# More features looked up on TensorE, fewer gathered, in a DLRM interaction tower

## The reference

```python
e = jnp.stack([tbl_0[ids[:, 0]], ..., tbl_26[ids[:, 26]]], axis=1)    # (2048, 27, 128)
dots = jnp.einsum('bnd,bmd->bnm', e, e)
r, c = np.tril_indices(27, k=-1)
h = jnp.concatenate([dots[:, c, r], dense_ctx], axis=1)               # (2048, 367)
h = jnp.maximum(h @ W_top1 + b_top1, 0.0)                             # 512
h = jnp.maximum(h @ W_top2 + b_top2, 0.0)                             # 256
y = h @ W_top3                                                        # (2048, 1)
```

## Time and profile before

| | before |
|---|---|
| median of 3 runs | 397.31 us (397.29 to 397.81) |
| profiled execution | 396.33 us |
| its span | 394.4 us |
| mean granted TensorE clock | 0.97 of full speed |
| busy: PE, DVE, ACT, POOL | 325.2, 251.2, 148.8, 276.4 us |
| matmuls of look-ups, L415 | 1152 |
| indirect gathers, L386 | 288 |

### The profile page before, as it was taken

The page is one execution under the profiler, slowest core; times in us unless marked ns, Lnnn a source line. Parts: engine busy times, 40 slices in busy tenths (PEclk is TensorE's granted clock), DMA queues, the critical chain, the costliest instruction groups (busy, mean ns, idle before and its releaser), DMA issues.

```text
span 394.4 us, 13599 instructions
## 1 busy us (share of the span) xinstructions
PE 325.2 (82%) x5928; PEld 289.8 (73%) x5928; DVE 251.2 (64%) x518; ACT 148.8 (38%) x406; POOL 276.4 (70%) x295
## 2 busy tenths in 40 slices
PE   0751989998998799997989989898889889799947
PEld 0741979887787687896778877697778777797836
DVE  3744995997657836696656856686755856741531
ACT  2251434453433433433433343342533343343421
POOL 6777677777777777777777777777777777777200
PEclk9995799999999989999999999999999999999987
DMA  7996276343433323332533333332423333222100
GB/s 166 248 228 148 73 190 141 95 109 70 91 77 84 83 70 80 87 89 62 96 75 81 88 73 79 80 91 67 97 68 83 81 76 68 57 55 58 29 2 2
DMA packets 23990, 35.48 MB, mean 90 GB/s; under 512 B 7936, under 2 KB 17832, under 8 KB 23932
## 3 DMA queue, kind: packets, MB, share of 16 engines
q0 software_dynamic: 9216, 18.89, 23.1%
q1 hardware_dynamic: 14716, 15.73, 14.8%
HBM read 34.59 MB, written 0.01 MB: 88 GB/s over the span
## 4 chain that ended last, share of the span: by engine, by line
POOL 45%; PE 21%; issue 17%; DMA 9%; SPq 3%; DVE 3%; ACT 1%; DVEq 0%
POOL rows L386 45%; PE e_banks L415 8%; DMA ids_wide<-in_ids 5%; DMA rows<-in_tbl,idx 4%; PE w_bank L476 4%; PE g_banks L446 3%; PE e_banks L427 3%; PE w_bank L487 3%; SPq L339 2%; PE w_bank L465 1%; DVE one_hot L550 1%; DVE zt L561 1%; DVE h L246 1%; SPq L329 1%; ACT et L265 0%
## 5 line engine op out<-in xcount | busy, mean ns | idle before, releaser
L386 POOL DMA_INDIRECT rows<-in_tbl,idx x288 | 275.6, 957 | 91.4 <-issue 85.1
L550 DVE TENSOR_TENSOR one_hot<-ids_wide,row_no 125x1024 fp32r<-125x1024 int32 x144 | 168.5, 1216 | 94.1 <-PE e_banks L415 78.0
L415 PE MATMUL e_banks<-one_hot,table_hi 125*128 125x256 f32 x576 | 153.8, 303 | 27.6 <-DVE table_lo L541 24.3
L415 PE MATMUL e_banks<-one_hot,table_lo 125*128 125x256 f32 x576 | 146.6, 290 | 0.0
L415 PEld LDWEIGHTS e_banks<-one_hot,table_hi 125*128 125x128 f32 x576 | 114.2, 198 | 31.2 <-issue 28.4
L415 PEld LDWEIGHTS e_banks<-one_hot,table_lo 125*128 125x128 f32 x576 | 114.7, 199 | 0.0
L265 ACT ACTIVATE et<-e_banks 128x256 f32<-128x256 f32 x72 | 45.1, 626 | 121.7 <-PE e_banks L415 121.7
L256 ACT ACTIVATE et<-e_banks 128x512 f32<-128x512 f32 (+1 forms) x96 | 51.2, 551 | 45.7 <-PE e_banks L427 45.2
L427 PE MATMUL e_banks<-ident,rows 128*128 128x128 f32 x288 | 46.1, 279 | 22.4 <-DMA rows<-in_tbl,idx 22.4
L446 PEld LDWEIGHTS g_banks<-et 128*26 128x26 f32 x4096 | 43.5, 103 | 16.8 <-issue 13.8
L446 PE MATMUL g_banks<-et 128*26 128x26 f32 x4096 | 52.2, 191 | 3.6 <-issue 2.4
(11 more groups left out here) (19 smaller groups left out, 63.8 us busy)
## 6 DMA issues: line engine op xcount, KB each, us to landing
ids_wide<-in_ids SPq DMA_DIRECT2D x72, 125.0 KB
rows<-in_tbl,idx POOLq DMA_INDIRECT x288
et<-in_tbl SPq DMA_DIRECT2D x9, 448.0 KB
w<-in_W_top SPq DMA_DIRECT2D x2, 256.0 KB
w<-in_W_top SPq DMA_DIRECT2D x1, 512.0 KB
et<-in_tbl SPq DMA_DIRECT2D x9, 52.0 KB
w<-in_W_top SPq DMA_DIRECT2D x1, 222.0 KB
idx<-in_idx SPq DMA_DIRECT2D x1, 202.5 KB, 3.0
```

The lines of the kernel that those rows point to most:

```text
L386: pool.indirect_dma_start(rows[:, k % RING, a, :], None, tables[f], bass.IndirectOffsetOnAxis(ap=idx[:, t, f:f + 1], axis=0)).then_inc(row ...
L415: last = nc.tensor.matmul(e_bank[n % E_BANKS][:, 0:UNIT], part[:, q, c, :], one_hot[:, hot_slot(o, piece), c % PIECE, :], start=(c == 0 an ...
L550: nc.vector.tensor_tensor(one_hot[:, hot_slot(o, piece), :, :], ids_wide[:, o % IDS_RING, :].unsqueeze(1).broadcast_to([OP, PIECE, UNIT]), ...
```

## The change

- Eleven features are looked up (7 and 16 are new) and sixteen gathered, in four chunks of four a tile; the ring of chunks has seven places. A tile is four ticks.
- Features are renumbered in `et`: gathered ones first, looked-up ones behind them, so that each chunk is drained by one copy. The pitch of a sample in `et` is 27 elements in place of 32. The order of the pairs in `h` follows, and W_top1's rows are permuted to it outside the kernel, where the kept tables are padded to 128 partitions of eight rows and stacked as well.
- The triangle is cut into seven rectangular blocks in place of 26 rows: three are copied on ScalarE, four on VectorE.
- `z`, `zt` and `a2` are single, no longer double.
- The drains of H and L1 are all on ScalarE, but for the last unit.
- Each table is one DMA. The eleven ids of unit 0 are issued beside their tables; seven of them land in space of `a1T` and `hT` that is not yet in use. The second part of `idx` comes behind the third table.
- The schedule: look-ups of a unit are spread over ticks ahead of its tiles, grams go two steps to a tick, and H follows the turn of its second tile by one tick.

```diff
-ONE_HOT = (3, 4, 14, 19, 22, 23, 24, 25, 26)
-LOOK_UP_AT = (-5, -4, -3, -2, 0, 1, 2, 3, 4)
+LOOKED_UP = (3, 4, 7, 14, 16, 19, 22, 23, 24, 25, 26)
+GATHERED_IN = ()
-RING = 6
+RING = 7
...
+def pair_blocks(NF):
+    blocks = []
+    half = 1 << (NF - 1).bit_length() - 1
+    while half:
+        whole = [a for a in range(0, NF, 2 * half) if a + 2 * half <= NF]
+        if whole:
+            blocks.append((len(whole), half, half, half, 0, 2 * half))
+        rest = len(whole) * 2 * half
+        if rest + half < NF:
+            blocks.append((1, NF - rest - half, half, rest + half, rest, 0))
+        half //= 2
+    return blocks
...
+    AHEAD = 2
+    FIRST = [("OH", 0, q) for q in looked_up(0)[:AHEAD]]
+    for n, q in enumerate(looked_up(0)[AHEAD:]):
+        put(n * TILE_AT[PAIR] * 7 // 8 // FIRST_LOOK_UPS, ("OH", 0, q))
+    LOOK_UPS_FROM = [0] + [TILE_AT[PAIR * u] * 3 // 4 for u in (1, 2)] + [TILE_AT[PAIR * (u - 1)] + 2 for u in range(3, UNITS + 1)]
     for u in range(1, UNITS):
+        first, next_first = LOOK_UPS_FROM[u:u + 2]
+        for n, q in enumerate(looked_up(u)):
+            put(first + n * (next_first - first) // len(looked_up(u)), ("OH", u, q))
     for t in range(LAST_TILE - 1):
-        at = CHUNKS * (t + 1)
-        for p in range(G_PIECES):
-            put(at + p, ("G", t, p))
-        put(at + G_PIECES, ("turn", t), ("pack", t))
-    for u in range(LAST - 1):
-        at = PAIR * CHUNKS * (u + 1) + CHUNKS
-        layers(u, BOTH, at + 2, (at + 3, at + 4, at + 4, at + 4), at + 9)
+        at = TILE_AT[t + 1] + (2 if t == 0 else 0)
+        put(at, ("G", t, 0), ("G", t, 1))
+        put(at + 1, ("G", t, 2), ("G", t, 3), ("turn", t), ("pack", t))
+    for u in range(LAST):
+        at, then = TILE_AT[PAIR * (u + 1)] + 2, TILE_AT[PAIR * (u + 1) + 1] + 2
+        put(at, *[("H", u, c, BOTH) for c in range(KC)], ("L1", u, 0, BOTH))
+        put(at + 1, ("L1", u, 1, BOTH), ("L1", u, 2, BOTH), ("L1", u, 3, BOTH))
+        put(then - 2 * (u == LAST - 1), ("L2", u, 0))
+        put(then + 1 - 3 * (u == LAST - 1), ("L2", u, 1))
...
-        et = sb("et", [P, ET_TILES, P, STRIP])
-        z = sb("z", [P, PAIR, STRIP, NP])
-        zt = sb("zt", [P, PAIR, NP, STRIP])
+        et = sb("et", [P, ET_TILES, P, NF])
+        z = sb("z", [P, STRIP, NP])
+        zt = sb("zt", [P, NP, STRIP])
...
-            return "act" if s[2] % 2 == 0 else "dve"
+            return "dve" if s[1] == LAST and s[2] % 2 == 1 else "act"
...
-            for q in range(NOH):
-                if q < IDS_RING:
-                    load_ids(q)
-                load_table(q)
+            for n, q in enumerate(TABLE_ORDER):
+                if n < FIRST_LOOK_UPS:
+                    load_ids(n)
+                load_table(n)
+                if n == 2:
+                    sp.dma_start(idx[:, 1:TILES, :], idx_in[:, 1:TILES, :]).then_inc(idx_rest, 16)
+            for o in range(FIRST_LOOK_UPS, FIRST_LOOK_UPS + IDS_RING):
+                load_ids(o)
...
             def turn_tile(t):
                 dve.wait_ge(g_drained, 2 * (t + 1))
+                if t > 0:
+                    dve.wait_ge(act_packed, (KC - 1) * t)
+                    dve.wait_ge(dve_packed, t)
```

More of the change, by code:

```diff
@@ L39, in dlrm_tower @@
     assert B % UNIT == 0 and TILES > ET_TILES
[L41 to L46, removed]
+    assert kept_tables.shape[0] == P and OC % PIECE == 0
     PIECES = OC // PIECE
@@ L61, in dlrm_tower, with looked_up, places_gathered @@
     LAST_TILE = TILES - 1
[L64 to L79, removed]
+    ORDER = feature_order(NF)
+    GATHERED = NF - NOH
+    def looked_up(u):
+        return range(1 if u in GATHERED_IN else 0, NOH)
+    def places_gathered(t):
+        return GATHERED + (t // PAIR in GATHERED_IN)
+    PLACES = {}
+    for t in range(TILES):
+        n = places_gathered(t)
+        parts = -(-n * P // BANK)
+        sizes = [n // parts + (i < n % parts) for i in range(parts)]
+        for i in range(parts):
+            PLACES[t, i] = range(sum(sizes[:i]), sum(sizes[:i + 1]))
+    CHUNKS = list(PLACES)
+    CHUNK_AT = {chunk: k for k, chunk in enumerate(CHUNKS)}
+    TICKS = len(CHUNKS)
+    TILE_AT = [CHUNK_AT[t, 0] for t in range(TILES)] + [TICKS]
+    LOOK_UPS = [(u, q) for u in range(UNITS) for q in looked_up(u)]
+    LOOK_UP_NO = {look_up: o for o, look_up in enumerate(LOOK_UPS)}
+    FIRST_LOOK_UPS = len(looked_up(0))
     BOTH = (0, 1)
@@ L122, in dlrm_tower @@
+    put(at, *[("G", t, p) for p in range(G_PIECES)], ("turn", t), ("pack", t))
+    put(at + 2, *[("H", LAST, c, (0,)) for c in range(KC)], *[("L1", LAST, m, (0,)) for m in range(M1)])
+    put(at + 3, ("L2", LAST, 0))
+    put(TICKS, *[("G", LAST_TILE, p) for p in range(G_PIECES)], ("turn", LAST_TILE), ("pack", LAST_TILE),
+        *[("H", LAST, c, (1,)) for c in range(KC)], *[("L1", LAST, m, (1,)) for m in range(M1)], ("L2", LAST, 1))
     RANK = ("G", "OH", "turn", "pack", "H", "L1", "L2")
@@ L144, in h_turned @@
         return W_AT["H", u, KC - 1, w_tiles(u, j)] + 1
+    BLOCKS, at = [], 0
+    for block in pair_blocks(NF):
+        BLOCKS.append((at, block))
+        at += block[0] * block[1] * block[2]
+    assert at == PAIRS
+    ACT_BLOCKS = sum(at < 2 * P for at, _ in BLOCKS)
+    FIRST_COLUMN = BLOCKS[0][1][3] - 1
+    assert BLOCKS[0][1][0] == 1 and BLOCKS[1][0] >= P
     dense_v = dense_ctx.rearrange("(u j p) c -> p u j c", j=PAIR, p=P)
@@ L230, in rows_landed @@
         def rows_landed(k):
-            return 16 * sum(len(FEATS[c % CHUNKS]) for c in range(k % RING, k + 1, RING))
+            return 16 * sum(len(PLACES[CHUNKS[c]]) for c in range(k % RING, k + 1, RING))
         def hot_slot(o, piece):
@@ L249, in drain_t @@
             _, t, i = s
[L250 to L257, removed]
+            n, at = E_AT[s], PLACES[t, i]
+            act.wait_ge(t_filled, CHUNK_AT[t, i] + 1)
+            nc.scalar.activation(et[:, t % ET_TILES, :, at[0]:at[-1] + 1],
+                                 e_bank[n % E_BANKS][:, 0:len(at) * P].rearrange("p (f b) -> p b f", b=P), ACT.Copy
+                                 ).then_inc(e_drained[n % E_BANKS], 1)
         def drain_look_up(act, s):
@@ L276, in drain_grams @@
                                  ).then_inc(g_drained, 1)
[L279 to L316, removed]
-                nc.vector.tensor_scalar(out, cols, b1[:, m:m + 1], 0.0, ALU.add, ALU.max
-                                        ).then_inc(w_drained[n % WB], 1)
+        def pack_block(eng, j, at, block):
+            count, columns, rows_of, first_column, first_row, step = block
+            first = zt[:, first_column - 1:first_column - 1 + columns, first_row:first_row + rows_of]
+            out = h[:, j, at:at + count * columns * rows_of]
+            if count == 1:
+                return copy(eng, out.rearrange("p (c r) -> p c r", r=rows_of), first)
+            if rows_of == 1:
+                src = zt[:, :, :].rearrange("p c r -> p (c r)")
+                src = src[:, (first_column - 1) * STRIP + first_row:][:, ::step * (STRIP + 1)]
+                return copy(eng, out, src[:, 0:count])
+            whole = zt[:, :, :].rearrange("p c r -> p (c r)")
+            return copy(eng, out.rearrange("p (k c r) -> p k c r", c=columns, r=rows_of), diagonal(whole, block))
@@ L384, in _ @@
                     pool.wait_ge(t_filled, k - RING + 1)
-                for a, f in enumerate(FEATS[i]):
+                for a, place in enumerate(PLACES[t, i]):
+                    f = ORDER[place]
                     pool.indirect_dma_start(
@@ L614 @@
     placed = ids.reshape(B // P, QUADS, STRIP, NF)
-    arrays = {"in_" + name: np.ascontiguousarray(inputs[name]) for name in inputs if name not in ("ids", "b_top1")}
+    order = feature_order(NF)
+    on_chip = LOOKED_UP if not GATHERED_IN else LOOKED_UP[1:]
+    kept = ["ids", "b_top1", "W_top1"] + [f"tbl_{f}" for f in on_chip]
+    arrays = {"in_" + name: np.ascontiguousarray(inputs[name]) for name in inputs if name not in kept}
     arrays["in_idx"] = np.ascontiguousarray(placed.transpose(2, 1, 0, 3)).reshape(P, B // P, NF)
@@ L618 @@
     arrays["in_b1"] = np.ascontiguousarray(np.asarray(inputs["b_top1"]).reshape(-1, P).T)
+    tables = np.stack([np.asarray(inputs[f"tbl_{f}"]) for f in LOOKED_UP])
+    tables = np.pad(tables, ((0, 0), (0, P * OC - tables.shape[1]), (0, 0)))
+    arrays["in_kept_tables"] = np.ascontiguousarray(tables.reshape(len(LOOKED_UP), P, OC, -1).transpose(1, 0, 2, 3))
+    w1 = np.asarray(inputs["W_top1"])
+    pairs = [sorted((order[a], order[b])) for a, b in pair_order(NF)]
+    w1_rows = [b * (b - 1) // 2 + a for a, b in pairs] + list(range(len(pairs), w1.shape[0]))
+    arrays["in_w1"] = np.ascontiguousarray(w1[w1_rows])
     nc = bacc.Bacc("TRN2", target_bir_lowering=False, num_devices=1)
```

283 lines of the change are left out of this document (179 added, 104 removed).

## The result

The changed kernel takes 387.78 us (386.12 to 388.44, four runs) against 397.3: a ratio of 0.9752, interval 0.972 to 0.9785. Measured again, with later experiments, it took 389.1 us, 0.9809 (0.9769 to 0.9849); so where two kernels were not measured together, a difference of half a per cent says nothing. It is faster, as forecast, and inside the range, but by 9.5 us where 20 were forecast. The profiled execution took 386.12 us with a span of 384.3.

The account below looks back on a forecast made before the run. POOL's gathers were taken to bound the kernel, PE close behind. PE's path of 315.3 us, +24.7 for look-ups, -4.0, -5.1, -7.8, -0.9, gave 322.2; with 4 for stalls, 48 of start and the median's distance, 377 us; range 366 to 391.

Parts of the forecast that it names:

- pack and turn: Tile's turn and pack before H: 3.6 us on DVE and ACT, covered by PE's 4.2 us in all units but the first.
- the step on transposes and chunks: Four chunks a tile for five: 38 fewer transposes, -4.0 us, and 30 fewer gram boundaries at 0.17 us each, -5.1 us.
- if a gram step is over 0.9 us: One of the signs given in advance that would show the prediction wrong: a gram step on PE over 0.9 us.
- its 0.77 us: Gram step on PE, taken from start to start at 0.77 us, with no change from the new pitch.
- The tail: End of the kernel: about 21 us before, 0.9 us less through a shorter last pack; a tail of 20 us expected.
- the step on layers: H and L1 drains move to ACT except in the last unit; the wait at L1 costed at zero, -7.8 us.
- the drains of the e banks: In ACT's queue: what stands behind a waiting pack; the pack was held covered, by 0.6 us only.
- the L1 wait: PE's last L1 step of a unit waits 1.26 us for a DVE drain behind one-hots, 7.8 us in all; expected gone.
- The 4 us added for stalls: Allowance on PE's path since row-wait slack is gone; from 52 to 90 us PE idled 1.7 us of 38.
- The case of helpers that starve PE: Rival: lateness of DVE's one-hots or ACT's drains falls on PE, +10 to +17 us, 387 to 394 us; chance 0.20.
- the start's bound by transfer: End of unit 0's eleventh look-up by transfer: 7.26 MB there at 46 us, plus 1.1 + 1.2 + 2.1, given as 50.7 us.
- the chance of the range: Chance given to 366 to 391 us, the forecast plus the starved case's lower half: about 0.75 to 0.8.

Follow-up runs that it names:

- f4: Changed kernel without the matmuls of the tables' lower parts, so looked-up embeddings are only the upper parts: 358.19 us, 0.9029 of the kernel before.
- h2: Changed kernel with features 7 and 16 gathered again, nine looked up and eighteen gathered, in five chunks a tile: 393.03 us, 0.9904 of the kernel before.
- e1: Changed kernel with a look-up put between the two gram steps of a tick: 386.3 us, 0.9721 of the kernel before.
- e2: Changed kernel with all four gram steps of a tile in one tick: 415.33 us, 1.0463 of the kernel before.
- h1: Changed kernel with H's third chunk and L1's first step a tick later, and long matmuls mixed into the tail's grams: 379.86 us, 0.9541 of the kernel before.
- f3: Changed kernel with the drains of L1's second and fourth step on DVE again, H still on ACT: 388.96 us, 0.9791 of the kernel before.
- e3: Changed kernel with H's middle chunk drained by DVE again, layer 1 still on ACT: 416.8 us, 1.0517 of the kernel before.
- g4: Changed kernel with the weights loaded two ticks later, measured in the state of long pauses: 0.9234 of the kernel before.

## Why the prediction was off by half the gain

Right: PE took over from POOL, as f4 shows; row waits went; the start ended at 48.4 us for 48; 77 look-ups cost 149 us for 150.5; pack and turn kept their cover. The move of work from gathers to look-ups gains by itself 1.0 to 1.5% (h2), as much as all the rest of the change or more.

Wrong, in the step on transposes and chunks: "each such boundary costs 0.17 us", booked as -5.1 us for 30 fewer of them. With its waits a gram step cost 0.965 us before (57.9 us by 60) and 1.0 us after; the waits in front of single steps came back inside the pairs. The term measures +2.2 us, not -5.1: this is the largest miss, 7.3 us in a total of 10.7. e1 shows that the placing matters little up to pairs (0 to 3.5 us), e2 that it does beyond. The prediction's own sign, "if a gram step is over 0.9 us", was met, but the kernel before met it already: its 0.77 us left out part of the waits. The tail, with four steps in a row, was sized at 20.2 us and took 22.4.

Wrong, in the step on layers: "on ACT only 0.4 to 0.7 us drains stand in front". Three stood there, behind a pack; H cost 3.9 us more. The prediction named "the drains of the e banks" as what waits behind a pack, and not H's own. h1 gives this back and more.

Right in size for the wrong reason: the L1 wait of 7.8 us went, but f3 shows that the choice of engine is not why. The prediction had misread the wait: the drain stood behind a turn and its packs, and not behind one-hots alone, and the new order moved the turn.

The 4 us added for stalls were not met: transposes and L1 took 2.0 us more and look-ups and L2 2.2 less. They hid as much of the misses above. The rest is 0.4 us of start, 0.6 of the median's distance from the span, and rounding.

The case of helpers that starve PE had the right place (ACT behind the pack), but that place gave 3.9 us where the case had 10 to 17. That its time, 387 to 394 us, fits is luck, and so is that the range holds the measured time: most of the miss is in grams and tail, which the case does not name. Two small sums of the prediction are off: the start's bound by transfer adds up to 50.4 us, not 50.7, and the chance of the range, 0.62 and half of 0.20, is 0.72, not 0.75 to 0.8.

## What to carry to other kernels

A saving booked for fewer boundaries has to be read from the cost of a whole step, waits included, and not from the wait that stands in front of it. When drains move to one engine, write down its queue at that moment, beginning with the wait at its head. And when one engine becomes the bound, a schedule edit of one tick (H's third chunk) can be worth nearly as much as the change itself.

## What the runs showed of the hardware

Short matmuls can outrun what feeds PE its instructions. In a run of grams a load with its matmul of 26 columns takes 0.011 us (112 in 1.27 us). Two steps in a row cost as two, about 1 us each; four in a row bring pauses of up to 2.6 us, in the stretch shown of e2 after 160 loads. The page has a queue that fits (packets, MB, share of 16 engines; the changed kernel):

```profile
q8 instruction: 49, 0.80, 0.8%
```

Its packets are 16 KB each, and their number follows PE's loads and matmuls: 49 for 12,304 of them, 47 for 11,856 in the kernel before, 43 for 10,896 in f4, one for some 252. In e2 all thirteen pauses of 1 us or more inside or in front of grams end 1.25 to 1.52 us after such a packet has landed, though the packets come 7 to 8 us apart on average; the three of the changed kernel end 1.31 to 1.42 us after one. In the twelve traces of the usual state it is 41 of 43 pauses. So these pauses end with a refill of PE's instructions. An estimate from these numbers: at full pace grams use up a packet's 252 loads and matmuls in 1.4 us, while the next one needs 0.9 us at the least to land and 1.25 more until PE runs. No run changed the refilling itself, so the cause is read from the times and not tried.

A pause costs more than itself: after 2.13 us of it in e2 loads came 0.21 us apart for 2 us, and the granted clock was 0.66; after 2.82 us in e3 it was 0.63, and loads came 0.22 us apart.

The state in which every kernel takes 1.6 to 1.7 times as long is something else. The same 49 packets are read there, but of g4's 48 pauses of 1 us or more at grams only 4 end 1.2 to 1.6 us after one. g4 has 166.8 us of "issue" at grams where the changed kernel has 19.5, and a mean granted clock of 0.80 where it has 0.98; both together make the time. What brings this state about stays open; one chip showed it in one set of runs and not in the next.
